# Layer 2's steps in another order: scores and exponentials of the newest batch first, turn and weighing of older batches behind them

## The reference, cut to what matters

```python
def _L2_xattn_ref(query, key, value, Wq, Wk, Wv, Wo):    # 32 heads of 16, 8 key/value heads
    q = (query @ Wq)...   k = (key @ Wk)...   v = (value @ Wv)...
    scores = jnp.einsum('bhqd,bhkd->bhqk', q, k) * scale
    probs = jax.nn.softmax(scores, axis=-1)
    out = jnp.einsum('bhqk,bhkd->bhqd', probs, v)
    return out.transpose(...).reshape(b, sq, DIM) @ Wo
x = x + _L1_ffn_ref(_layernorm(x), L1_ffn_weight, L1_ffn_bias)
x = x + _L2_xattn_ref(_layernorm(x), ctx_4096, ctx_4096, ...)
x = x + _L2_ffn_ref(_layernorm(x), L2_ffn_A, L2_ffn_B, L2_ffn_Wr)
```

## Time and profile before

| | us |
|---|---|
| median of 3 runs (1667.07 to 1669.41) | 1669.07 |
| the profiled execution | 1672.39 |
| its span, first to last instruction | 1670.6 |
| TensorE busy in the span | 1577.3 |
| VectorE, ScalarE, GpSimd busy | 823.0, 754.4, 518.0 |

### The profile page before, as it was taken

How to read it: one execution, slowest core, us unless ns; L and a number is a source line. 1 busy time by engine, 2 the same in 40 slices (tenths; PEclk the granted TensorE clock), 3 DMA queues, 4 the chain that set the end, 5 groups by cost and what they waited for, 6 DMA issues and landing times. The chain is left out here.

```text
span 1670.6 us, 25988 instructions
## 1 busy us (share of the span) xinstructions
PE 1577.3 (94%) x9522; PEld 1282.7 (77%) x9522; DVE 823.0 (49%) x1697; ACT 754.4 (45%) x2529; POOL 518.0 (31%) x648
## 2 busy tenths in 40 slices
PE   7998998789999999999999998878999999999998
PEld 5877777678888888888888887655555578888876
DVE  3555666445444355554444435765565412333455
ACT  3544444444444454545454555444343211454552
POOL 5666564232222222222222223333232100123333
PEclk8999998999999999999999999998999999999999
DMA  8000000102001010101010110001100000222111
GB/s 237 14 7 7 8 1 14 51 2 95 26 4 47 15 38 26 39 26 39 26 39 26 39 51 1 1 29 51 39 1 1 20 9 11 69 73 74 47 31 60
DMA packets 45678, 58.22 MB, mean 35 GB/s; under 512 B 26368, under 2 KB 33920, under 8 KB 42736
## 3 DMA queue, kind: packets, MB, share of 16 engines
q1 hardware_dynamic: 43872, 56.05, 10.6%
q10 hardware_dynamic: 1616, 0.51, 0.1%
q0 software_dynamic: 64, 0.00, 0.0%
HBM read 48.94 MB, written 2.10 MB: 31 GB/s over the span
## 5 line engine op out<-in xcount | busy, mean ns | idle before, releaser
L1747 ACT ACTIVATE big<-pb 128x128 f32<-128x128 f32 x384 | 106.6, 278 | 312.3 <-PE pb L807 203.0
L2110 POOL TENSOR_TENSOR big<-big 128x512 f32<-128x512 f32 x96 | 99.9, 1041 | 260.9 <-DVE big L1392 260.9
L1798 ACT ACTIVATE big<-pb,big 128x128 f32<-128x128 f32 x384 | 136.1, 368 | 64.3 <-issue 41.6
L1387 DVE TENSOR_REDUCE big<-pb 128x4 f32<-128x512 f32 x96 | 65.8, 686 | 180.0 <-PE pb L846 171.5
L822 PE MATMUL pb<-wkh,CXh 128*128 128x256 f32 x512 | 149.3, 292 | 1.5 <-DVE big L1377 1.5
L822 PE MATMUL pb<-wkl,CXh 128*128 128x256 f32 x512 | 144.3, 282 | 0.0
L822 PE MATMUL pb<-wkh,CXl 128*128 128x256 f32 x512 | 143.6, 281 | 0.0
L2100 POOL TENSOR_SCALAR big<-big 128x6 f32<-128x6 f32 x64 | 13.1, 204 | 419.3 <-ACT big L1747 419.0
L1180 DVE TENSOR_TENSOR X<-X,pb 128x512 f32<-128x512 f32 x128 | 86.9, 679 | 85.5 <-PE pb L1028 41.5
L871 PE MATMUL pb<-woh,oh 128*128 128x512 f32 x256 | 112.6, 440 | 8.0 <-DVE X L1180 5.0
L807 PE MATMUL pb<-wqh,CXh 128*128 128x512 f32 x256 | 102.1, 399 | 5.8 <-DVE big L1357 4.4
(11 more groups left out here) (255 smaller groups left out, 3979.2 us busy)
## 6 DMA issues: line engine op xcount, KB each, us to landing
big<-in_w SPq DMA_DIRECT2D x17, 1024.0 KB, 4.9
big<-in_w SPq DMA_DIRECT2D x24, 256.0 KB, 2.9
big<-in_w SPq DMA_DIRECT2D x8, 512.0 KB, 3.5
o<-o SPq DMA_DIRECT2D x96, 32.0 KB, 1.9
X<-in_x SPq DMA_DIRECT2D x8, 256.0 KB, 7.4
big<-in_cn SPq DMA_DIRECT2D x8, 256.0 KB, 3.1
CXlf<-in_cT SPq DMA_DIRECT2D x8, 256.0 KB, 5.0
big<-in_wa SPq DMA_DIRECT2D x1, 2048.0 KB, 7.9
```

What stands on the lines that cost most here:

```text
L1387: v.tensor_reduce(m[j % 2], quarters(bank(p)), AX, MAX, negate=True).then_inc(S.m, 1)
L1747: y = a.activation(sq[i % 2], bank(p)[:, j * width:j * width + 128], ACT.Square, accum_out=ss[i % 2][:, first + j:first + j + 1])
L1798: y = a.activation(e_[:, c], bank(p)[:, c], ACT.Exp, bias=m[j % 2][:, k:k + 1], scale=1.0, accum_out=z[j % 2][:, k:k + 1])
L2110: g.tensor_tensor(quarters(e_), quarters(e_), bc(r[j % 2], 128), MUL).then_inc(*on.to(S.pn))
```

## The change

In the list of `pipe2`, `l2_s` and `l2_e` move ahead of the turn and the weighing, and the turn ahead of the weighing. Before, the order within a step was `l2_v`, `l2_t`, `l2_s`, `l2_z`, `l2_a`, `ffn1`, `l2_e`. After, it is `l2_s`, `l2_e`, `l2_t`, `l2_v`, `l2_z`, `l2_a`, `ffn1`. How many steps a stage is behind does not change, and no stage is added or removed.

```diff
-    pipe2 = batch_steps(16, [("f2_rows", 7, odd), ("l3_rows", 12, odd), ("f2_o", 11, odd),
-                             ("l3_stats", 11, odd), ("f2_b", 9, odd), ("l2_c", 6, odd), ("f2_stats", 6, odd),
-                             ("l2_v", 5, every), ("l2_t", 4, every), ("l2_s", 2, every), ("l2_z", 3, every),
-                             ("l2_a", 1, every), ("ffn1", 0, every), ("l2_e", 2, every), ("l2_q", 0, queries_at), ("f2_a", 8, odd),
+    pipe2 = batch_steps(16, [("f2_rows", 7, odd), ("l3_rows", 12, odd), ("f2_o", 11, odd), ("l3_stats", 11, odd),
+                             ("f2_b", 9, odd), ("l2_c", 6, odd), ("f2_stats", 6, odd), ("l2_s", 2, every),
+                             ("l2_e", 2, every), ("l2_t", 4, every), ("l2_v", 5, every), ("l2_z", 3, every),
+                             ("l2_a", 1, every), ("ffn1", 0, every), ("l2_q", 0, queries_at), ("f2_a", 8, odd),
                              ("f2_h", 8, odd), ("f2_turn", 7, odd), ("l3_turn", 12, odd)])
```

## The result

The changed kernel takes 1676.15 us (median of 4 runs, 1675.27 to 1680.04) against 1669.03 for the kernel before (4 runs beside it): ratio 1.005, 95% interval 1.0032 to 1.0067, so 5.3 to 11.2 us slower. 1674.1 was predicted. The profiled execution took 1675.27, its span is 1673.5.

A forecast was written before the change was run, and what follows sets the result against it. Early layer-2 steps wait on a chain (scores, VectorE, GpSimd's multiplications, mask); from step 9 TensorE bounds. Terms -0.1 + 0 + 3.2 + 1.8 + 0.1 = +5.0 us on 1669.07 give 1674.1, range 1669.2 to 1678.0.

The forecast's parts named there:

- The stretch: Layer 2, from its first scores to its last output projection: +5.0 us in all.
- step 6: Scores of batch 4 to first output projection: turn and weighing now stand before the query projections, +1.2 us.
- ScalarE costs nothing: Exponentials ahead of the turn's copies: delayed copies are needed a step later or more; -0.1 us.
- Steps 3 to 5, sum 0: First scores to those of batch 4: 1.0 us gained, then given back; 0, bounds -0.6 to +0.6.
- step 8: Batch 6's scores to second output projection: turn and weighing follow the scores at half clock, +2.6 us.
- Rival 3: Longer waits before scores in steps 5, 6 and 8 lower the clock on projections: +8.2 us, 1677.3; chance 0.14.
- First projection to batch 6: Step 7, first output projection to the scores of batch 6: -0.6 us, those scores starting 0.6 late.
- The pairs, +1.8 and 0.1: Steps 10 to 17: four pairs at 0.45 us each for VectorE's copy, 1.8; last two projections 0.1.
- Behind layer 2, 0: The tail, from layer 2's last output projection to the end: no change, 0 us.
- Rival 1: Layer 2: delays do not add up, four pairs free and step 8 at full clock; +2.2 us, 1671.3; chance 0.24.
- Rival 2: Layer 2: earlier scores shorten every loop if VectorE's copy, not the mask, is free; -3.6 us, 1665.5; chance 0.10.

The follow-up runs named there:

- r5: The changed kernel with ScalarE put back to the old order: 1678.63 us, 1.0052 of the kernel before.
- r4: The kernel before with only ScalarE in the new order: 1675.84 us, 1.0045 of the kernel before.
- r6: The kernel before with GpSimd's key mask moved ahead of its two multiplications: 1673.23 us, 1.001 of the kernel before.
- r10: GpSimd's mask first throughout; new order in steps 0 to 8, from step 9 weighing, scores, exponentials, turn: 1660.28 us, 0.9945 of the kernel before.
- r8: The changed kernel with VectorE's copy of the weighed result moved behind sum and reciprocals: 1683.81 us, 1.0081 of the kernel before.
- r7: The changed kernel with GpSimd's key mask moved ahead of its multiplications: 1662.61 us, 0.9959 of the kernel before.
- r2: The kernel before with only TensorE in the new order: 1687.07 us, 1.0103 of the kernel before.
- r3: The kernel before with only VectorE in the new order: 1680.44 us, 1.0061 of the kernel before.
- r9: Old order in steps 0 to 8, new order from step 9, on all engines: 1673.37 us, 1.0021 of the kernel before.

## Why the prediction was right, and where it wasn't

The direction and the mechanism hold. The stretch came out at +5.3 for +5.0, but that it is so near is luck: step 6 was 1.8 us short, and of this 1.6 was covered by terms that came out lower (by 0.7, 0.5, 0.1 and 0.3). One term outside, behind layer 2, was missing, and with it the median is +7.1.

*ScalarE costs nothing.* True in the changed kernel from step 9 on (r5: 152.93 against 152.90), open in the light steps. The reason given, that its copies are needed a step later, was too short: with the weighing still in front the same move costs 6.0 us (r4). It is free because the weighing moved last.

*Steps 3 to 5, sum 0.* -0.7, a little outside the bounds of 0.6. The scores of batch 2 came 1.0 earlier, as expected; but of this only 0.3 was given back. The copy did start late and in the loop (1128.89, behind a wait of 0.68), and wait and copy cost 1.1 us where 0.9 was taken. Two things gave back 0.8. VectorE got these scores 1.6 us after their start and not 2.1, for they ran partly at the full clock (1.59 us). And the reading of the loop before was a little off: there the scores stood behind a turn that waited for the second multiplication,

```profile
1137.13 1.11 PE L963 MATMUL pb<-ident,big 128*128 128x128 f32 x4 [0.19 <-POOL big L2144]
```

and started 0.35 us after the mask had ended (1137.83 to 1138.18), not as soon as it had; after, it is 0.06 (1133.28 to 1133.34). That the mask did not close the loop alone is also what r6 shows.

*Step 6, +1.2.* This is the step that failed: +3.0, because I took turn and weighing at the full clock. They stand behind a wait of 3.40 us and run at 1.2 GHz in all three profiles: 2.91 us from start to start instead of 1.60, 1.3 of the missing 1.8; the rest is the scores ahead of them and the two short turns behind, also at the lower level. At the full clock, in r5, the term comes out as predicted. The argument that put step 8 at half clock held for step 6 as well, and I did not apply it. Rival 3 had this, in another place: it put the lower clock on the projections, and they ran at the full one (7.07 us).

*First projection to batch 6.* -1.1 where -0.6 was expected. Steps 3 to 7 together: +0.6 foretold for the start of batch 6's scores, +1.25 measured.

*Step 8, +2.6.* +2.5. The idle time ahead was put at about 5 us and is 5.07.

*The pairs, +1.8 and 0.1.* +1.6. The projection waits 0.2 us for the copy instead of 0.3 to 0.5, and the next scores 0.26 for the mask. A pair is 0.32 to 0.38 us longer, 1.4 in all; the last two intervals have 0.2 together. By the Trainium skill, Perfetto Trace Analysis, section Identifying the Most-Contended Engine, weight loads at 52 of 100 us spoke for room in which this would vanish; it did not, and r10, with 53.57 us of weight loads, has TensorE busy for 99.99 of 100. Here the trace's rows decide against the rule.

*Behind layer 2, 0.* +1.7 from one fall of the clock, which comes in every profile of the changed kernel and in neither of the kernel before. It was in no term.

Rival 1 (+2.2) would need step 8 at the full clock and free pairs; neither is so. Rival 3 named projections that run at the lower level as well; none does in the changed kernel, but two do in r8 and cost 1.7 us each, so it was a fair price for another order. Rival 2 (faster) was to decide if the copy were free; r8 shows that it is not, in either place. But its core, that scores which start sooner shorten every loop behind them, comes true as soon as the mask no longer ends the wait (r7). The prediction had the mask in its loop and did not draw the conclusion: GpSimd's order was the one that the change left alone.

## What to carry to other kernels

On an engine that works in order, work that is ready belongs ahead of an instruction that waits: moved behind it, turn and weighing cost their full time and, behind the idle time, at half the clock. Putting the newest batch first pays only if all that it needs comes first too: find the instruction that ends the wait (the Trainium skill, Perfetto Trace Analysis, section Optimization Strategy, says to ask what blocks the gap; the waits above agree) and move that one, here GpSimd's 0.61 us mask ahead of 2.23 us of multiplications. And an order that several engines share can't be judged by its parts: alone they cost 18.4, 8.9 and 6.0 us, together 5.3.

## What the runs showed of the hardware that was not expected

The falls of the granted clock came again in every profile of the same kernel (three of the changed one, two of the one before) and moved from kernel to kernel. In step 6 an idle time of 3.40 us was followed by 1.2 GHz in three profiles of the changed kernel (12.60 to 12.68 us) and by 2.4 GHz in r5 (10.17). In r8 a wait of 1.93 us ahead of a projection was followed by a fall (5.40 us), and a wait of 1.92 ahead of the next one was not (3.70). In the tail the longer of the two waits shown (2.00 us) is not the one with the fall behind it. Six profiles have tails of 355.3 to 355.8 (before twice, r2, r3, r8, r10) and eight 357.0 to 357.5 (after three times, r4, r5, r6, r7, r9), with nothing between. The waits ahead overlap: 1.67 to 2.00 us where the tail is short, 1.81 to 2.23 where it is long. Neither the length of the stretch nor any one engine's order goes with it; what decides stays open. It means that a change of a few tenths of a per cent may gain or lose 1.7 us hundreds of microseconds behind the place that it touches.
